# Down-projection by seven products instead of eight, in units of 256 tokens, with keys and values kept in memory

## The reference

```
q    = layer_norm(x) @ wq + bq;   k, v = context @ wk + bk, context @ wv + bv
p    = softmax(q k^T / sqrt(32) + causal mask over the 64 keys)
x1   = x + (p v) @ wo + bo
out  = x1 + gelu(layer_norm(x1) @ w1 + b1) @ w2 + b2
```

## Time and profile before

| | |
|---|---|
| median of 3 runs | 1852.21 us |
| profiled execution | 1853.13 us, span 1851.3 us |
| granted TensorE clock, mean | 0.986 |
| busy: TensorE, VectorE, ScalarE, GpSimd | 97%, 67%, 35%, 24% |

### The profile page before, as it was taken

One profiled execution on the slowest core, in us unless ns is written; L12 is line 12 of the kernel. 1 busy time (PEld: TensorE's weight loads), 2 busy tenths in 40 slices (PEclk: granted clock), 3 DMA queues, 4 the chain that ended last, 5 costly groups with the idle time before them and its releaser, 6 DMA issues.

```text
span 1851.3 us, 26679 instructions
## 1 busy us (share of the span) xinstructions
PE 1798.9 (97%) x10261; PEld 820.7 (44%) x10261; DVE 1244.7 (67%) x1926; ACT 644.0 (35%) x803; POOL 445.3 (24%) x378
## 2 busy tenths in 40 slices
PE   6769999999999999999999999999999999999999
PEld 3324444444444444444444444444444444444444
DVE  6876877676775768667576766757686575866622
ACT  5654433242332424233242423324242232424211
POOL 3512232031411214131231313213151221413200
PEclk8789999999999999999999999999999999999999
DMA  8240232323042232404123140322414033241200
GB/s 290 52 125 1 58 80 57 81 46 92 1 92 46 51 87 35 96 8 89 49 46 92 26 88 24 72 66 46 92 24 87 28 64 74 46 92 24 46 23 23
DMA packets 287931, 116.55 MB, mean 63 GB/s; under 512 B 262552, under 2 KB 264384, under 8 KB 287808
## 3 DMA queue, kind: packets, MB, share of 16 engines
q1 hardware_dynamic: 287808, 114.87, 27.8%
HBM read 31.22 MB, written 16.78 MB: 26 GB/s over the span
## 4 chain that ended last, share of the span: by engine, by line
PE 91%; DVE 5%; DMA 2%; ACT 1%; POOL 1%; issue 1%; SPq 1%; DVEq 0%; ACTq 0%
PE ff_ps L1190 35%; PE ff_ps L1456 34%; PE at_ps L1190 17%; PE at_ps L1349 3%; PE at_ps L1389 1%; DVE w_all L874 1%; ACT arena L664 1%; DMA w_all<-in_L_xattn_w 0%; DMA arena<-in_L_xattn_wk 0%; DVE arena L1110 0%; PE ff_ps L1262 0%; POOL arena L585 0%; DVE arena L874 0%; DVE smax L1108 0%; DVE arena L1163 0%
## 5 line engine op out<-in xcount | busy, mean ns | idle before, releaser
L1190 PE MATMUL ff_ps<-arena,w_all 128*128 128x512 f16 x3072 | 702.8, 381 | 7.2 <-DVE w_all L874 3.2
L1456 PE MATMUL ff_ps<-w_all,arena 128*128 128x512 f16 x3072 | 699.5, 380 | 3.2 <-DVE w_all L874 3.2
L1190 PEld LDWEIGHTS ff_ps<-arena,w_all 128*128 128x128 f16 x3072 | 300.2, 98 | 377.3 <-issue 18.6
L1456 PEld LDWEIGHTS ff_ps<-w_all,arena 128*128 128x128 f16 x3072 | 294.7, 98 | 361.7 <-issue 11.4
L797 ACT ACTIVATE arena<-ff_ps,b1p,scales 128x512 f32<-128x512 f32 x256 | 198.7, 776 | 624.7 <-PE ff_ps L1190 621.9
L1163 DVE TENSOR_SCALAR arena<-arena,scales 128x512 f16<-128x512 f32 x256 | 150.3, 587 | 205.8 <-ACT arena L797 205.7
L874 DVE SCALAR_TENSOR_TENSOR arena<-arena,scales 128x512 f16<-128x512 f32 x256 | 239.3, 935 | 9.1
L535 POOL TENSOR_TENSOR rstd<-ve,minus_half 128x1 f32<-128x1 f32 x128 | 85.8, 670 | 563.4 <-DVE ve L846 563.4
L580 POOL TENSOR_TENSOR x_sb<-x_sb,bo_row 128x512 f32<-128x512 f32 x64 | 92.6, 1478 | 361.5 <-PE at_ps L1349 361.5
L729 ACT ACTIVATE norm_hl<-xhat 128x512 f16<-128x512 f32 x120 | 74.0, 628 | 286.0 <-DVE xhat L863 286.0
L585 POOL TENSOR_TENSOR arena<-arena,rsum 128x1024 f32<-128x1024 f32 x64 | 124.8, 1970 | 179.6 <-DVE rsum L1136 179.6
(11 more groups left out here) (162 smaller groups left out, 1364.1 us busy)
## 6 DMA issues: line engine op xcount, KB each, us to landing
x_sb<-in_x SPq DMA_DIRECT2D x64, 256.0 KB, 2.8
out_x<-arena SPq DMA_DIRECT2D x64, 256.0 KB, 2.1
w_all<-in_L_xattn_w SPq DMA_DIRECT2D x6, 1024.0 KB, 11.7
arena<-in_L_xattn_w SPq DMA_DIRECT2D x2, 1024.0 KB, 15.6
v_sb<-v_sb SPq DMA_DIRECT2D x6, 256.0 KB, 3.7
arena<-in_ctx SPq DMA_DIRECT2D x1, 1024.0 KB, 5.8
arena<-in_L_xattn_wk SPq DMA_DIRECT2D x1, 1024.0 KB, 8.0
arena<-in_L_xattn_wq SPq DMA_DIRECT2D x1, 1024.0 KB, 7.8
```

Source lines behind the costliest of these rows:

```text
L1190: last = nc.tensor.matmul(out_ap, s, m, start=(i == 0), stop=(i == n - 1))
L1456: last = nc.tensor.matmul(ff2_ps[:, t, :], pair[:, s, rows], m[:, j], start=(j == 0 and i == 0), stop=(j == NJ - 1 and i == 2))
```

## The change

1. The down-projection takes pairs of hidden blocks, pairs of token tiles and the two halves of the 512 output columns as a 2x2 by 2x2 product, and does it with Strassen's seven products instead of eight. The unit is 256 tokens by 256 hidden columns. A slot has 16 units: half h of the tokens (units 0 to 7, then 8 to 15). The up-projection of a unit is 24 matmuls of 256 columns, the down-projection 7 x 3 = 21 matmuls of 256 columns.
2. The factors of the products are sums of GELU blocks. GELU runs twice per unit on 256 columns; GpSimd makes five blocks of sums from four (`factor_sums`: three instructions of 256, 256 and 128 elements per partition); in the next group ScalarE writes the high half of seven blocks (896 elements) and VectorE the low half.
3. Products are gathered from PSUM by six additions per half (`drain`), on VectorE; `drain(0)` stands at the head of group 11 and `drain(1)` after the last group.
4. `g_pair` has three buffers of seven blocks. `norm_hl` has two buffers instead of four: the high half of tile t waits until tile t-2 has been transposed.
5. GpSimd walks through the groups as well; its steps have letters in `PLAN` now (b, B: add bo, b2; M: normalise; R, r: rstd), and several steps moved: D, N, A and C are spread over positions 25 to 32.
6. Keys and values are written to memory in slot 0 and each batch's share is loaded by SyncE (four and two DMAs per batch, after the h transposes of the slot before), instead of lying in SBUF.
7. w2 is loaded once for its magnitudes and, for two quarters, again for the conversion; all magnitudes are taken in slot 0. In slot 1 each w2 unit is summed by GpSimd (`weight_sums`) and converted in four parts of 512, 512, 512 and 256 elements.

The core of the diff:

```diff
-    25: [("O", 0), ("O", 1), ("G", 0), ("O", 2), ("G", 1), ("D", 0), ("O", 3), ("G", 2), ("D", 1),
-         ("G", 3), ("D", 2), ("D", 3)],
-    27: [("N", 0), ("N", 1), ("N", 2), ("N", 3)],
-    29: [("A", 0), ("A", 1), ("C", 0), ("A", 2)], 30: [("C", 1), ("A", 3), ("C", 2)], 31: [("C", 3)],
+    25: [("O", 0), ("R", 0), ("O", 1), ("R", 1), ("G", 0), ("O", 2), ("R", 2), ("G", 1), ("D", 0), ("O", 3),
+         ("R", 3), ("D", 1)],
+    26: [("G", 2)], 27: [("D", 2), ("G", 3), ("N", 0), ("r", 0), ("N", 1), ("r", 1)],
+    28: [("D", 3), ("N", 2), ("r", 2), ("N", 3), ("r", 3)],
+    29: [("A", 0), ("A", 1), ("C", 0)], 30: [("C", 1), ("A", 2)], 31: [("C", 2), ("A", 3)], 32: [("C", 3)],
...
# ScalarE, the norm steps
-                        wait(act, q_moved[t] if kind == "G" else h_moved[t], 16 * c)
-                    nc.scalar.activation(norm_hl[:, t, 0], xhat[:, t % 2], ACT.Copy).then_inc(n_hi, 1)
+                    if kind == "G":
+                        act.wait_ge(q_moved[t + 2] if t < 2 else h_moved[t - 2], 16 * c)
+                    elif t >= 2:
+                        act.wait_ge(q_moved[t - 2], 16 * c + 16 * ahead)
+                    elif kind == "A":
+                        wait(act, h_moved[t + 2], 16 * c)
+                    nc.scalar.activation(norm_hl[:, t % 2, 0], xhat[:, t % 2], ACT.Copy).then_inc(n_hi, 1)
...
# ScalarE, head of each group
-                        nc.scalar.activation(gelu_full[g % 2], ff1_ps[:, g % 2, :], ACT.Gelu,
-                                             bias=b1p[:, g:g + 1], scale=col(C1)).then_inc(g_full, 1)
+                        for odd in range(2):
+                            at, j = 7 * P * odd, 2 * (g % NU) + odd
+                            last = nc.scalar.activation(factors[g % 2][:, at:at + HALF],
+                                                        ff1_ps[:, g % 2, odd * HALF:(odd + 1) * HALF], ACT.Gelu,
+                                                        bias=b1p[:, j:j + 1], scale=col(C1))
+                        last.then_inc(g_full, 1)
+                    if ff and 1 <= g <= NJ:
+                        u = g - 1
+                        act.wait_ge(g_sum, 3 * NJ * c + 3 * (u + 1 - NJ))
+                        wait(act, ff2_done, NJ * c + (u + 1 - NG - NJ))
+                        nc.scalar.activation(g_pair[u % NG][:, 0], factors[u % 2][:, FACTORS], ACT.Copy, scale=col(SG)
+                                             ).then_inc(g_hi, 1)
...
# GpSimd
+                def factor_sums(u):
+                    pool.wait_ge(g_full, NJ * c + (u + 1 - NJ))
+                    f = factors[u % 2].rearrange("p (s n) -> p s n", n=P)
+                    nc.gpsimd.tensor_tensor(f[:, 3:5], f[:, 0:2], f[:, 7:9], ALU.add).then_inc(g_sum, 1)
+                    nc.gpsimd.tensor_tensor(f[:, 5:7], f[:, 0:9:8], f[:, 1:8:6], ALU.subtract).then_inc(g_sum, 1)
+                    nc.gpsimd.tensor_tensor(f[:, 2], f[:, 1], f[:, 7], ALU.add).then_inc(g_sum, 1)
...
# VectorE
+                def drain(h):
+                    blocks = x1[1 - par][:, 2 * h:2 * h + 2].rearrange("p t (s n) -> p (t s) n", s=2)
+                    done = 12 * c + (6 * h - 12)
+                    dve.wait_ge(ff2_done, NJ * c + (NU * (h + 1) - NJ))
+                    dve.wait_ge(x1b_set, 4 * c + (2 * h - 2))
+                    def add(n, into, products, factor):
+                        if n:
+                            dve.wait_ge(out_set, done + n)
+                        nc.vector.scalar_tensor_tensor(into, products, col(factor), into, ALU.mult, ALU.add
+                                                       ).then_inc(out_set, 1)
+                    add(0, blocks[:, 1:3], twice(0, 0), C2)
+                    add(1, blocks[:, 1::2], twice(0, 1), C2)
+                    add(2, blocks[:, 0::3], both(1), C2)
+                    add(3, blocks[:, 1:3], both(1), C2M)
+                    add(4, blocks[:, 1:3], both(2), C2)
+                    add(5, blocks[:, 0:3:2], twice(3, 0), C2)
                 for g in range(GROUPS):
+                    if ff and g == NU + LAG:
+                        drain(0)
                     if attn:
                         for kind, t in plan(c, 2 * g):
                             step(kind, t)
                     aside(c, 2 * g)
-                    if ff and g < NJ:
-                        dve.wait_ge(g_full, NJ * c + (g + 1 - NJ))
-                        pair = g_pair[g % NG]
-                        nc.vector.tensor_scalar(pair[:, 0, :], gelu_full[g % 2], col(SG), None, ALU.mult
-                                                ).then_inc(g_hi, 1)
-                        dve.wait_ge(g_hi, NJ * c + (g + 1 - NJ))
-                        low(pair[:, 1, :], gelu_full[g % 2], col(SG), pair[:, 0, :], g_lo)
+                    if ff and 1 <= g <= NJ:
+                        u = g - 1
+                        dve.wait_ge(g_hi, NJ * c + (u + 1 - NJ))
+                        pair = g_pair[u % NG]
+                        low(pair[:, 1], factors[u % 2][:, FACTORS], col(SG), pair[:, 0], g_lo)
...
# TensorE, down-projection of unit u = g - 3, half h
+                        for m in PRODUCTS:
+                            bank, side = PLACES[m]
+                            opens, closes = m in (1, 2, 4, 6), m in (0, 3, 5, 6)
+                            if u % NU == 0 and opens:
+                                wait(pe, out_set, 12 * c + (6 * h - 18 + BANK_DRAINED[bank]))
+                            for i, (s, a) in enumerate(((0, 0), (0, 1), (1, 0))):
+                                last = nc.tensor.matmul(
+                                    ff2_ps[:, bank, side * HALF:(side + 1) * HALF], pair[:, s, m * P:(m + 1) * P],
+                                    w2_units[:, u % NU, m, a], start=(u % NU == 0 and opens and i == 0),
+                                    stop=(u % NU == NU - 1 and closes and i == 2))
```

More of the change, by code:

```diff
@@ L503, in slot @@
                             load_x(c, t)
+                        if first and t == 1:
+                            store_values(2)
+                            store_values(3)
+                            load_w2(1)
                         if t and not first:
@@ L510, in slot @@
                     sp.wait_ge(o_ps, 4 * c + TT)
+                    if after is not None:
+                        sp.wait_ge(s_ps, 4 * c + TT)
+                        sp.wait_ge(v_ps, 4 * c + TT)
+                        if isinstance(c, int) and c == 1:
+                            sp.wait_ge(kT_stored, 16)
+                            for n in range(KT):
+                                sp.wait_ge(v_stored[n], 16)
+                        load_keys(kT_d[:, :, :, bass.ds(after * SC, SC)], kblk_loaded)
+                        load_values(v_d[bass.ds(after * SC, SC)])
                     for t in range(TT):
@@ new lines, in step @@
+                def step(kind, t):
+                    if kind == "b":
+                        add_bo(t)
+                    elif kind == "B":
+                        add_b2(t)
+                    elif kind == "M":
+                        normalise(t)
+                    elif kind == "R":
+                        rstd_of(c, TT + t)
+                    elif kind == "g":
+                        rstd_of(c, t)
+                    elif kind == "r" and not (isinstance(c, int) and c == NCHUNK - 1):
+                        rstd_of(c + 1, t)
@@ L782, in _, with slot @@
             magnitudes(W_O, 2)
-            magnitudes(W_1, 3)
-            magnitudes(W_1 + 1, 4)
-            def slot(c, par, attn, ff, batch):
+            for n in range(2):
+                feed_forward_sums(n)
+            def slot(c, par, attn, ff, batch, after=None):
                 first = isinstance(c, int) and c == 0
@@ L815, in slot @@
                             outputs_scaled()
-            slots(act, slot, loads=True)
+            slots(act, slot)
         @block.vector
@@ L880, in convert, with convert_unit @@
                 low(lo, src, scale, hi, conv_lo)
+            def convert_unit(u):
+                for part in range(4):
+                    dve.wait_ge(w2_hi_set, 4 * u + part + 1)
+                    low(w2_units[:, u, W2_PARTS[part], 1], w2_part(u, part), col(A2),
+                        w2_units[:, u, W2_PARTS[part], 0], w2_lo_set)
             def maximum_rows(n):
@@ L1171, in slot @@
                 if ff:
-                    for t in range(TT):
-                        dve.wait_ge(ff2_done, 4 * c + (t + 1 - TT))
-                        if t == 0:
-                            dve.wait_ge(x1b_set, 4 * c)
-                        old = x1[1 - par][:, t]
-                        nc.vector.scalar_tensor_tensor(old, ff2_ps[:, t, :], col(C2), old, ALU.mult, ALU.add
-                                                       ).then_inc(out_set, 1)
-            slots(dve, slot, loads=True)
+                    drain(1)
+            slots(dve, slot)
         @block.tensor
```

498 lines of the change are left out of this document (262 added, 236 removed), and 13 rows, old and new, of tables (PLAN, PLAN_FIRST).

## The result

The changed kernel takes 2041.69 us (median of 4 runs, 2039.22 to 2045.13) where the kernel before took 1852.44 beside it: 1.102 times as long (95% interval 1.1005 to 1.1032). The forecast was 1880, with 1815 to 1910 as its range. The direction was right; the loss is 189 us and not 28.

The account below looks back on a forecast made before the run. Bound: TensorE's in-order stream. Profiled 1853.1 - 67.8 (stream) + 49 (slot ends) + 35 (drain(0)) + 9 (slots 0 and 1) + 3.9 (kernel end) = 1882, 1881 against the median; predicted 1880 us, range 1815 to 1910.

Parts of the forecast that it names:

- place two: At drain(0), mid-slot: the late drain stalls TensorE at down-projection 8 by 2.5 us in 14 slots, +35 us.
- place one: End of a slot: TensorE stalls 3.8 us for unit 15's low half, slots 2 to 14, +49 us.
- slot 1's conversions: Slot 1: w2's larger conversion takes 10 us more on VectorE, of which its idle time takes about half.
- TensorE's stream: All 16 slots: matmuls of 256 columns take 109.2 ns, saving 4.24 us per slot, -67.8 us.
- Rival (c): Shared port of VectorE and GpSimd: both stalls grow by 1 us, +27, 1909 us; clock may suffer too; chance 0.08.
- Place three: Start and end of the kernel: +9 us for slots 0 and 1, +3.9 at the end, key and value DMAs 0.
- The late norms behind slot 1: Slot 1's norms at positions 35 to 37 delay slot 2's first down-projection: 9.5 us lost.
- (a): Rival: only the end of the slot stalls, drain(0) finds VectorE free; 1847 us; chance 0.19.
- (b): Rival: neither the slot's end nor drain(0) stalls, latencies being shorter; 1798 us; chance 0.16 with what lies between.
- (d): Rival: matmuls of 256 columns take 118 ns, +70, 1950 us; chance 0.03 together with (e).
- (e): Rival: the seven products cost as eight in the down-projection, +5.2 us per slot; chance 0.03 together with (d).
- The end of the kernel: After the last group: six drain additions stand alone where one did, +3.9 us.

Follow-up runs that it names:

- experiment 12: Four-buffer kernel of experiment 9 with GpSimd's additions of bo and b2 moved from positions 0 to 9 to 7 and 22: 1954.6 us.
- experiments 1: Changed kernel with steps A2, C2, A3, C3 of the next norm moved behind unit 15 (position 33): 2008.8 us.
- 9: Changed kernel, drain(0) one group earlier, A0, A1, C0 at position 31, C1 at 32, tiles 2, 3 at 33: 1981.1 us (two buffers), 1967.2 (four).
- (7): Changed kernel with four norm buffers again and ScalarE's waits as in the kernel before: 2038.6 us.
- (4): Changed kernel with dummy matmuls filling TensorE's idle time ahead of down-projections 8, 14 and 15 in slots 2 to 15: 2022.2 us.
- experiment 11: Four-buffer kernel of experiment 9 with seven eighths of GpSimd's sums left out (GELU blocks in slots 2 to 16, w2 in slot 1): 1898.2 us.
- (6): Changed kernel with seven eighths of GpSimd's sums of w2 left out in slot 1, from the second unit on: 2029.0 us.
- experiment 5: Changed kernel with seven eighths of GpSimd's sums of GELU blocks left out in slots 2 to 16: 1969.7 us.
- experiment 10: GELU-block sums of slots 2 to 16 on VectorE: 2010.1 us on the early-drain kernel with all norms behind unit 15, 2009.7 on experiment 9's four-buffer kernel.

## Why the prediction was off, by its own steps

The step that failed first and cost most is one link of place two: "GELU 10, high half of 9 until 36.5". It let ScalarE go on at once, as if GpSimd's sums of unit 9 were done. In the trace they weren't, ScalarE waited 2.57 us for them, and the place cost 7.4 us and not 2.5. The other terms that were too small are place one (1.9 us per slot), slot 1's conversions, and the waits at Q and O, which the sum had at nothing.

- **TensorE's stream**: right. 109.2 ns per 256 columns, -4.24 us per slot. An unstalled slot of 104.7 us was the prize; the best that a kernel with all the work reached here is 112.9, in some slots of experiment 12 (113.6 on average).
- **Place one**: found, its last link wrong, its size too small. The text had VectorE pile up (D, N, A, C before the low halves), and then A2 waiting for tile 0's transpose with unit 15's high half behind it. The pile-up is real (experiments 1, 9). The wait is real too, 1.88 us, but taking it away gives 3 us in all (7). VectorE's low half of unit 14 took 1.6 in place of 1.15 and was over just before the transpose landed. The prediction reached 33.4 for the end of low(15) from the first O matmul; in the trace it is 1237.48 - 1202.19 = 35.3. Of the 1.9 between, 1.4 are there when C0 ends (A0's and A1's norms take 0.95 in place of 0.54, C0 0.94 in place of 0.69), and 0.3 more when tile 0's transpose has landed. These 1.9 are the whole miss of the place; the slower matmuls behind unit 14 add nothing to it (4).
- **Place two**: the right wait with the wrong size, 7.4 in place of 2.5. It is the term that failed most, 68 of the 157 us between the sum and the profiled execution. The text's chain holds to within 0.4 us up to GELU 10, which ends where it should, at 35.6 (from the first score matmul). Then the high half of 9 waits until 38.2, for two reasons that the text left out. GpSimd takes its steps in the order of the table, where the normalisation M3 stands before the sums of unit 9: they begin 1.7 us after GELU 9 has ended. And I took the sums at 1.9 us; alone they take 1.83, and their mean is 2.7. But just here they take 4.6, beside L2 and L3, which take 3.41 in place of 2.43. GpSimd's M3 and its three instructions for unit 9, VectorE's L2 and L3, ScalarE's high half behind them and the late low 9, in the kernel after:

```profile
1178.94 1.90 POOL L617 TENSOR_TENSOR arena<-arena,row_stats 128x1024 f32<-128x1024 f32 x1
1180.80 1.57 POOL L630 TENSOR_TENSOR arena<-arena 128x256 f32<-128x256 f32 x1
1182.33 1.71 POOL L631 TENSOR_TENSOR arena<-arena 128x256 f32<-128x256 f32 x1
1184.00 1.43 POOL L632 TENSOR_TENSOR arena<-arena 128x128 f32<-128x128 f32 x1
...
1181.70 3.41 DVE L960 SCALAR_TENSOR_TENSOR qT<-arena,qT 128x1024 f16<-128x1024 f32 x2
1186.54 1.20 DVE L960 SCALAR_TENSOR_TENSOR arena<-arena,scales 128x896 f16<-128x896 f32 x1 [1.42 <-ACT arena L889]
1187.66 4.67 DVE L1256 SCALAR_TENSOR_TENSOR arena<-ff_ps,scales,arena 128x512 f32<-128x512 f32 x6
...
1185.46 1.04 ACT L889 ACTIVATE arena<-arena,scales 128x896 f16<-128x896 f32 x1 [2.57 <-POOL arena L632]
```

  By these numbers (an estimate) either reason alone would have cost less: sums of 1.83 from 1180.80 on are done when GELU 10 ends, and sums of 4.6 without M3 before them make the high half wait 0.8. Together they are 2.6 of the 4.9 us by which the place was missed; the slower matmuls are 2.0 (4). The text's "if drain(0) ran on an idle VectorE it would cost 0.1" was tested by no run: in experiment 11 VectorE is in L2 and L3 until 1.8 us after down 7, and TensorE waits 1.5 for the drain. In slot 16 of the changed kernel, which has no attention, the drain begins 1.1 us after down 7, behind a low half, and TensorE loses 1.4.
- **Rival (c), port and clock**: both happened on top of the stalls. I gave it 0.08 and 1 us per stall, because the sum had used durations of instructions that ran alone. It was too small in both parts: stretched instructions make up most of place one's 1.9 and, with M3, place two's 2.6, and the clock is 2.0 at place two. Leaving out the sums saved 72 us, but that is their own time and their contention together; how much of it is contention was not separated. Holding the clock saved 20.
- **Place three**: the late norms behind slot 1 were right (9.5 forecast, 8.63 idle before slot 2's third up-projection, 10.2 with the slower matmuls); TensorE's wait there is for GELU 0, which stands on ScalarE behind the norms. Slot 1's conversions were not: "of which its idle time takes about half" overlooked that w1's and w2's low halves have a due time each, and that GpSimd's sums would stretch them. 36 us, of which 13 belong to the sums of w2 (6).
- **Q and O**: not seen, 27 us. Q waits 0.89 for ScalarE, where its step stands behind GELU and a high half that waits for GpSimd; O waits 0.69 for V's low half.
- **Rivals (a), (b), (d), (e)**: out. Both places stall, the matmuls stand 109.2 ns apart, and the down-projection of a unit has 21 of them. The end of the kernel was forecast at 3.9 and cost 6: 1.4 of the difference is drain(0) in slot 16, which the sum left out. TensorE doesn't wait for low 15 there.

## What to carry to other kernels

When a step adds a link on GpSimd next to a busy VectorE, price both engines' instructions stretched, at the worst place and not at the mean, and write down what stands before the new link in GpSimd's own queue. The sum of busy times won't show it: only TensorE was above 69%. And a wait that the trace shows isn't yet a cost. Take away what it waits for, and see what is late next: here the same two norm buffers were worth 0.2 us per slot in one order of the steps, hardly to be told from nothing, and 1.1 in another.

## What the runs showed of the hardware

- VectorE and GpSimd stretch each other. `low` of 896 elements: 1.15 alone, 1.41 on average; of 1024: 1.22 and 1.75; GpSimd's sum of 256: 0.72 and 0.94, up to 1.7. With the sums cut (experiment 5), the low half of 1024 is back at 1.24, but that of 896 only at 1.38; with the sums on VectorE (experiment 10) it is at 1.15. The drain, which reads one operand from PSUM, stays at 0.75 in every kernel, and GpSimd beside it at 0.72. The Trainium skill (SBUF — State Buffer, Who interferes with whom) says that a VectorE instruction with two inputs in SBUF contends with a GpSimd instruction that reads SBUF. By that rule the drain is spared; the trace agrees.
- GpSimd's `tensor_tensor` in float32, undisturbed, takes 0.45 us for 128 elements, 0.72 for 256 and 1.27 for 512.
- After waits of 2.5 and 4.1 us the next 21 matmuls took 3.92 and 4.87 us in place of 2.46, and during the latter the granted clock was 0.50, the lower of its two levels (1.2 GHz). With the gaps filled by dummy matmuls the granted clock was 1.00, unit 14 took 2.47, and unit 8 took 3.6, with a wait for the drain inside it.
